# Attention stage of a ViT tower: position products with the image innermost, GpSimd scaling the probabilities, a new order of TensorE's side jobs

## The reference

```python
qkv = (x @ qkv_w.T).reshape(b, n, 3, HEADS, HEAD_DIM).transpose(2, 0, 3, 1, 4)
q, k, v = (qkv[0], qkv[1], qkv[2])
attn = jnp.einsum('bhqd,bhkd->bhqk', q, k) * scale
r_p_k = tab_kv[iv] + tab_kh[ih]
attn = attn + jnp.einsum('bhqd,qkd->bhqk', q, r_p_k) * scale
attn = jax.nn.softmax(attn, axis=-1)
out = jnp.einsum('bhqk,bhkd->bhqd', attn, v)
r_p_v = tab_vv[iv] + tab_vh[ih]
out = out + jnp.einsum('bhqk,qkd->bhqd', attn, r_p_v)
out = out.transpose(0, 2, 1, 3).reshape(b, n, QKV_DIM)
return out @ proj_w.T + proj_b
```

## Time and profile before

| What | Value |
|---|---|
| median of 3 runs | 5148.42 us (5146.3 to 5152.68) |
| the profiled execution | 5149.14 us, its span 5147.4 us |
| TensorE busy | 4691.5 us, 91% of the span |
| VectorE, ScalarE, GpSimd busy | 3364.0, 2283.2, 562.3 us (65%, 44%, 11%) |
| mean granted TensorE clock | 0.954 of full speed |
| attention stage | from about 554 to 4034 us of the span |

### The profile page before, as it was taken

How to read it: one execution, slowest core, us unless ns; L and a number is a source line. 1 busy time by engine, 2 the same in 40 slices (tenths; PEclk the granted TensorE clock), 3 DMA queues, 4 the chain that set the end, 5 groups by cost and what they waited for, 6 DMA issues and landing times. The chain is left out here.

```text
span 5147.4 us, 91556 instructions
## 1 busy us (share of the span) xinstructions
PE 4691.5 (91%) x30810; PEld 4419.7 (86%) x30810; DVE 3364.0 (65%) x9549; ACT 2283.2 (44%) x6372; POOL 562.3 (11%) x530
## 2 busy tenths in 40 slices
PE   4775799899899989989989998998999699999999
PEld 4775599899889889989988998998999599999999
DVE  4555566666666766666666666676667477777776
ACT  2443555455555545545555555554554122222222
POOL 1122100000000000000000000000000133333333
PEclk8887799999999999999999999999999799999999
DMA  6452000000000000000000000000000100000000
GB/s 140 97 124 61 13 1 1 1 20 1 1 20 1 1 2 20 1 1 20 1 1 16 6 1 1 20 1 1 11 1 1 38 19 18 18 18 18 18 18 18
DMA packets 65157, 99.50 MB, mean 19 GB/s; under 512 B 3763, under 2 KB 60674, under 8 KB 61120
## 3 DMA queue, kind: packets, MB, share of 16 engines
q1 hardware_dynamic: 61312, 90.31, 7.0%
q0 software_dynamic: 944, 2.42, 0.3%
q10 hardware_dynamic: 2560, 2.36, 0.2%
HBM read 65.88 MB, written 29.20 MB: 18 GB/s over the span
## 5 line engine op out<-in xcount | busy, mean ns | idle before, releaser
L643 ACT ACTIVATE att_prob<-att_s,att_npeak 99x198 f32<-99x198 f32 x1536 | 640.1, 422 | 1221.4 <-DVE att_npeak L816 1175.5
L816 DVE TENSOR_REDUCE att_npeak<-att_s 99x2 f32<-99x396 f32 x768 | 436.0, 568 | 892.3 <-PE att_s L988 890.2
L971 PE MATMUL att_o<-att_probT,att_vx 99*96 99x198 f32 (+1 forms) x3072 | 683.2, 345 | 1.3 <-ACT att_probT L633 1.3
L988 PE MATMUL att_s<-att_kx,att_qx 96*99 96x198 f32 (+1 forms) x3072 | 657.4, 336 | 3.3 <-DVE att_xres L782 2.5
L1356 PE MATMUL ffn_y<-ffn_down,ffn_hidden 128*128 128x192 f32 x3564 | 634.8, 328 | 6.7 <-DVE ffn_acc L1268 4.8
L1356 PEld LDWEIGHTS ffn_y<-ffn_down,ffn_hidden 128*128 128x128 f32 x3564 | 585.6, 190 | 28.4 <-DVE ffn_acc L1268 27.4
L971 PEld LDWEIGHTS att_o<-att_probT,att_vx 99*96 99x96 f32 (+1 forms) x3072 | 509.5, 182 | 42.4 <-issue 32.7
L988 PEld LDWEIGHTS att_s<-att_kx,att_qx 96*99 96x99 f32 (+1 forms) x3072 | 517.1, 168 | 18.4 <-issue 4.4
L806 DVE TENSOR_SCALAR att_prob<-att_prob,att_total 99x198 f32<-99x198 f32 x1536 | 458.9, 342 | 26.9
L1134 POOL TENSOR_TENSOR ffn_hidden<-ffn_relu 128x384 f32<-128x384 f32 x462 | 379.4, 827 | 708.6 <-ACT ffn_relu L1163 400.2
L1163 ACT ACTIVATE ffn_relu<-ffn_h 128x384 f32<-128x384 f32 x231 | 113.3, 490 | 706.2 <-PE ffn_h L1345 705.9
(11 more groups left out here) (201 smaller groups left out, 9368.6 us busy)
## 6 DMA issues: line engine op xcount, KB each, us to landing
tok_pixels<-in_x SPq DMA_DIRECT2D x24, 1568.0 KB
ffn_hid<-hidden SPq DMA_DIRECT2D x34, 288.0 KB, 2.9
att_xres<-hidden SPq DMA_DIRECT2D x8, 1188.0 KB
hidden<-att_xres SPq DMA_DIRECT2D x8, 1188.0 KB
out_hidden<-ffn_acc SPq DMA_DIRECT2D x33, 288.0 KB, 2.3
hidden<-tok_rows SPq DMA_DIRECT2D x8, 1176.0 KB
att_oT<-in_L_attn_qkv_w ACTq DMA_DIRECT2D x1, 1536.0 KB, 11.4
tok_posb<-in_L_tok_pos_embedding POOLq DMA_DIRECT2D x1, 1176.0 KB, 42.6
```

Of the source, the lines that this page charges most:

```text
L643: ins = nc.scalar.activation(prob[:, i % 2, h, :], s_bank[i % 2][0:HALF, h * NTOK:(h + 1) * NTOK], ACT.Exp, bias=npeak[:, i % 2, h:h + 1], ...
L816: nc.vector.tensor_reduce(npeak[:, i % 2, :], s_bank[i % 2][0:HALF, 0:2 * NTOK].rearrange("p (h k) -> p h k", h=2), AX.X, ALU.max, negate= ...
L971: ins = nc.tensor.matmul(o_bank[j % 2][0:M, 0:NTOK], vx[:, p % 2, 2 * b + k, v0:v0 + M], probT[:, j % 2, k * NTOK:(k + 1) * NTOK], start=( ...
L988: ins = nc.tensor.matmul(s_bank[i % 2][0:HALF, h * NTOK:(h + 1) * NTOK], qx[0:K, p % 2, head, q0:q0 + HALF], kx[0:K, p % 2, head, b * NTOK ...
```

## The change

The kernel's parts that are edited, all in `attention_stage`:

- `q2` and `rx` now hold the image innermost (token 0 of 8 images, then token 1). ScalarE and VectorE write them at a distance of 8 values, `group_rhs` reads a grid row as 112 neighbours and a grid column as 14 runs of 8. The products lie in the bank in the same order, and the copies out of it (`by_image`, `by_image_cols`) read at distance 8.
- The table `tq` is padded from 64 to 72 columns.
- `scaled` becomes `inverted_sums`: VectorE only inverts; GpSimd scales both heads in one instruction. GpSimd's bias goes into 16 pieces, one behind the scaling in each of the first 16 steps of a group.
- ScalarE's `turned_out` comes ahead of the exponentials.
- `spread` orders the jobs anew and places them by a table of lengths, `COST`. The turns go between the Q and V jobs of the last unit, two of them into the unit before.
- `rowhot`, a helper of the setup, lies in the memory of `norm`.

```diff
-        tq = m.sb("tq", [128, NG, 64])
+        tq = m.sb("tq", [128, NG, WIDE])
...
-            return view(src, [[NTOK, GB], [step, n]], off)
+            return view(src, [[step * GB, n], [1, GB]], off * GB)
+
+        def by_image(src, n):
+            return view(src, [[1, GB], [GB, n]])
+
+        def by_image_cols(src, n):
+            return view(src, [[1, GB], [GB, SIDE], [SIDE * GB, n]])
...
+        COST = {"turn": [10] * TURN, "first": [9] * 8 + [8, 8, 8, 5] + [8, 8, 8, 4] + [18] * 4,
+                "last": [10, 9, 9, 6, 9, 9, 9, 5] + [7] * 8}
...
-                    jobs = f[:12] + l[:4] + f[12:14] + l[4:8] + f[14:17] + l[8:11] + f[17:] + l[11:]
...
-                    jobs = turns + f[:4] + l[:4] + f[4:9] + l[4:8] + f[9:14] + l[8:11] + f[14:17] + l[11:13] + f[17:] + l[13:]
...
+                if ending and not last:
+                    jobs = []
+                    for a in range(4):
+                        jobs += f(Q[a]) + (t(2 * a + 2) if a < 3 else []) + f(V[a]) + (t(2 * a + 3) if a < 3 else [])
+                    jobs += l(0) + f(R[0])
                 else:
+                    jobs = f(V[0], Q[0], V[1], Q[1], Q[2], V[2], Q[3]) + l(0) + f(R[0], V[3])
+                jobs += l(1) + f(R[1], K[0]) + l(2) + f(R[2]) + l(3) + f(R[3], K[1])
+                jobs += l(4) + f(C[0], K[2]) + l(5) + f(C[1]) + l(6) + f(K[3], C[2]) + l(7, 8) + f(C[3])
+                jobs += l(9, 10, 11, 12) + (t(0) if turning else []) + l(13, 14) + (t(1) if turning else []) + l(15)
+                begin = 5 if ending and last else 0
+                costs = [COST[kind][j] for kind, _, j in jobs]
                 for k, job in enumerate(jobs):
-                    between[p * UNIT + begin + k * (UNIT - begin) // len(jobs)].append(job)
+                    between[p * UNIT + begin + sum(costs[:k]) * (UNIT - begin) // sum(costs)].append(job)
...
+                def group(g, s):
+                    for i in range(STEPS):
+                        pool.wait_ge(inverted, g * STEPS + i + 1)
+                        nc.gpsimd.tensor_tensor(prob[:, i % 2, :, :], prob[:, i % 2, :, :],
+                                                view(total[:, i % 2, :], [[1, 2], [0, NTOK]]), ALU.mult).then_inc(probs, 1)
+                        if i < TILES:
+                            if i == 0:
+                                pool.wait_ge(norm_made, (g + 1) * TURN)
+                            ins = nc.gpsimd.tensor_tensor(xres[:, s, i, :], xres[:, s, i, :], pbias[:, :], ALU.add)
...
-                        nc.scalar.activation(q2[:, cols], bank[:, 0:HC], ACT.Copy, scale=SCALE)
+                        nc.scalar.activation(view(q2[:, :], [[1, HC // NTOK], [GB, NTOK]], j * HC // NTOK),
+                                             bank[:, 0:HC].rearrange("p (b n) -> p b n", n=NTOK), ACT.Copy, scale=SCALE)
...
+                        if v != "first" or i >= 2:
+                            turned_out(n, i)
                         act.wait_ge(peaks, n + 1)
...
-                        if v != "first" or i >= 2:
-                            turned_out(n, i)
...
-                    nc.vector.tensor_copy(rx[ext:ext + 32, p % 2, cols], o_bank[j % 2][ext:ext + 32, 0:NTOK]
+                    nc.vector.tensor_copy(view(rx[ext:ext + 32, p % 2, :], [[GB, NTOK]], b), o_bank[j % 2][ext:ext + 32, 0:NTOK]
...
-                    st.did(nc.vector.reciprocal(total[:, j % 2, :], total[:, j % 2, :]))
-                    st.settle()
-                    for h in range(2):
-                        ins = nc.vector.tensor_scalar(prob[:, j % 2, h, :], prob[:, j % 2, h, :],
-                                                      total[:, j % 2, h:h + 1], None, ALU.mult)
-                    ins.then_inc(probs, 1)
+                    nc.vector.reciprocal(total[:, j % 2, :], total[:, j % 2, :]).then_inc(inverted, 1)
```

More of the change, by code:

```diff
@@ L350, in attention_stage @@
     EXT = 32
+    WIDE = 72
     NG = 30
@@ L451, in spread, with t, f, l @@
             for p in range(PAIRS):
-                f = first_jobs(p + 1) if p + 1 < PAIRS or not last else []
-                l = last_jobs(p - 1) if p or not first else []
-                if p + 1 < PAIRS:
-                    jobs = f[:12] + l[:4] + f[12:14] + l[4:8] + f[14:17] + l[8:11] + f[17:] + l[11:]
-                    begin = 0
-                elif last:
-                    jobs, begin = l, 5
-                else:
-                    jobs = turns + f[:4] + l[:4] + f[4:9] + l[4:8] + f[9:14] + l[8:11] + f[14:17] + l[11:13] + f[17:] + l[13:]
-                    begin = 0
+                ending, turning = p + 1 == PAIRS, p + 2 == PAIRS and not last
+                def t(*js):
+                    return [("turn", NEXT, j) for j in js]
+                def f(*js):
+                    return [("first", p + 1, j) for j in js] if not ending or not last else []
+                def l(*js):
+                    return [("last", p - 1, j) for j in js] if p or not first else []
+                Q, K, R, C, V = (range(n, n + 4) for n in (0, 4, 8, 12, 16))
+                if ending and not last:
[3 more added lines that the diff above has]
+                    jobs += l(0) + f(R[0])
+                else:
+                    jobs = f(V[0], Q[0], V[1], Q[1], Q[2], V[2], Q[3]) + l(0) + f(R[0], V[3])
[4 more added lines that the diff above has]
+                costs = [COST[kind][j] for kind, _, j in jobs]
                 for k, job in enumerate(jobs):
-                    between[p * UNIT + begin + k * (UNIT - begin) // len(jobs)].append(job)
+                    between[p * UNIT + begin + sum(costs[:k]) * (UNIT - begin) // sum(costs)].append(job)
             return between
@@ L566, in _ @@
                 pool.wait_ge(consts_in, 16 * 5)
+                def group(g, s):
[7 more added lines that the diff above has]
+                            ins = nc.gpsimd.tensor_tensor(xres[:, s, i, :], xres[:, s, i, :], pbias[:, :], ALU.add)
+                            if i == TILES - 1:
+                                ins.then_inc(resid_made, 1)
                 with pool.Fori(0, GROUPS // 2) as pair:
                     for s in range(2):
-                        pool.wait_ge(norm_made, (pair * 2 + s + 1) * TURN)
-                        nc.gpsimd.tensor_tensor(xres[:, s, :, :], xres[:, s, :, :], view(pbias[:, :], [[0, TILES], [1, DIM]]),
-                                                ALU.add).then_inc(resid_made, 1)
+                        group(pair * 2 + s, s)
             @block.scalar
@@ L755, in job @@
                             ins = nc.vector.tensor_tensor(
-                                dst, view(bank[src:src + 32, :], [[n * SIDE, GB], [1, SIDE], [SIDE, n]]), dst, ALU.add)
+                                dst, by_image_cols(bank[src:src + 32, :], n), dst, ALU.add)
                     elif kind == "last" and j < 4:
@@ L772, in job @@
                         ins = nc.vector.tensor_tensor(
-                            dst, view(bank[:, :], [[n * SIDE, GB], [1, SIDE], [SIDE, n]]), dst, ALU.add)
+                            dst, by_image_cols(bank[:, :], n), dst, ALU.add)
                     elif kind == "last":
@@ L981, in group @@
                         if i % UNIT == 0:
-                            all_read(base, v, "first", p, FIRST - 1)
+                            all_read(base, v, "first", p, max(range(FIRST), key=lambda j: order[v]["first", p, j]))
                         K = 128 if head else 96
```

36 lines of the change are left out of this document (17 added, 19 removed).

## The result

The changed kernel takes 5074.59 us (median of 4 runs, 5065.28 to 5083.04) against 5147.36 us (4 runs, 5143.08 to 5152.68): ratio 0.9859, interval 0.9846 to 0.9871, so 73 us or 1.4% less. The forecast was 4990, 158 us less; the sign and the range held, the size was twice too large. The profiled execution took 5078.64 us, its span is 5076.9.

The account below looks back on a forecast made before the run. TensorE's own path of work, waits and clock was taken to bound the attention stage. Savings of 113 us in plain units, 43 in turn units and 5 elsewhere, less 3, gave 158 off 5149.1: 4990 us, range 4740 to 5090.

Parts of the forecast that it names:

- Image innermost: Position products on TensorE: column products fall from 0.195 to 0.10 us each, 5.1 us less a unit.
- writes into the bank become one run everywhere: Products' writes into PSUM become contiguous; no cost was given for strided writes into q2 and rx.
- 72 columns: Weights wider than 64 on TensorE: slower entry into five product runs goes, 0.9 to 1.0 us a unit.
- GpSimd scales: Scaling leaves VectorE, which loses 0.56 us a step; GpSimd's product takes 0.86 us, 3 us lost in all.
- rival 2: VectorE's normalises in the turns wait for GpSimd's product: 96 us at most, 5087 us in all; chance 0.07.
- ScalarE's order: Copy of transposed values ahead of the exponentials: ScalarE's jobs start 0.15 us later in a step.
- The plain unit: Sixteen attention steps without turns: 59.9 us of work plus 5.4 of waits, 65.3, saving 2.9 us each.
- named third-job waits: In a plain unit, jobs standing third or fourth wait for bank copies, 0.3 to 1.1 us each, 5.4 together.
- The unit ahead of the turns: The unit before the last of a group: two turns moved into it cost 0.7 us.
- The turn unit: Last unit of a group: work 62.0, waits 1.85, 8.1 and 6.5, sum 78.5, with the clock 85 us.
- The charge of 6.6 us for the clock: Turn unit: three gaps of 2.7 us lower the clock, charged 2.2 us each, half of 4.4.
- Rival 1: TensorE stays fed, earlier copies or full clock: plain units 62.0, turn units 70, 4758 us in all; chance 0.19.

Follow-up runs that it names:

- the filled unit: The changed kernel with eleven extra fp32 products ahead of each of Q1, Q2 and Q3 in the unit with the turns: 5052.93 us, 0.9813.
- plain writes: The changed kernel with q2 and rx written by image in one run, so its products read permuted tokens: 5003.00 us, 0.9725.
- the first two turns uncounted: The changed kernel with cost 0 for the first two turns in the table that deals jobs to steps: 5049.63 us, 0.9828.
- wait-free order: The changed kernel with jobs from a table, mostly two a step in a plain unit, turns spread over both last units: 4765.56 us, 0.9268.

## Why the prediction was right and wrong

- **Image innermost: right in its price, a cost missed.** 0.095 us a product for my 0.10, 0.195 before. That runs of 8 values go like one run is what follows from the rule on the page "SBUF — State Buffer" of the Trainium skill, under "cachelines"; the trace agrees. The step that failed is "writes into the bank become one run everywhere": I followed the writes into PSUM and not those into q2 and rx, which got the stride that the reads lost. This cost of 0.40 us a Q and 0.16 us a step had no term. Taking it away gives 5003 us, 13 from my 4990, and unit by unit 64.7 (forecast 65.3), 69.1 (66.0) and, as the mean of the six middle groups, 84.8 (85).
- **72 columns: right**, 1.0 us a unit, 29 us in all of 46, since the turn unit's clock took part of the rest.
- **GpSimd scales: right in size, not in weight.** 846 ns for 0.86; VectorE's normalises take 381 ns each (380 before), so the 96 us of rival 2 are not there, and the blocked scalings are gone with their instruction. The lock of the Trainium skill's page "SBUF — State Buffer", under "shared port pair", costs nothing that these rows show now. The bias pieces take 0.59 us, not 0.42, which nothing waits for. I never priced what the changed kernel would be without it: 207 us more.
- **ScalarE's order: wrong to leave it at 0.15 us of shift.** In the changed kernel it costs 29 us, through the last two units of a group.
- **The plain unit: right.** Each of the named third-job waits is there, within 0.35 us, and the sum missed by 0.5 us, less than the missed writes cost (1.1): the other terms were together too high by some 0.6.
- **The unit ahead of the turns: wrong.** I charged two turns, 0.7 us. It takes 4.6 to 5.8 us over a plain one: VectorE's normalises and low halves in front of its additions, the V job that slid into third place, and some clock.
- **The turn unit: waits right, clock wrong.** Q behind its turn waits 2.25 us (forecast 2.7), V0 2.4 (1.85), the later third jobs 6.3 together (6.5). The 78.5 us of work and waits are near the estimate of 79 at full clock from the filled unit. The charge of 6.6 us for the clock, half of 4.4 for each gap and so half a guess, was the term that failed: the six middle units average 91.3, some 12 above that estimate, about one of it the wait without a releaser. With plain writes they average 84.8, which the charge fits; most of the excess is thus a price of the missed writes. The unit took 84.06 us at a clock of 0.94 and 95.95 at 0.80, with the same waits. With shorter copies or filled waits no clock under 0.91 is left in the six groups; with ScalarE's old order one of 0.86 is, and with the first two turns uncounted one of 0.83. So all four make the low clock rarer, and only the first two kept it away in all six groups.
- **Rival 1** (4758, TensorE stays fed) fell for this order. The wait-free order comes to its time (4766) with the change's other parts, but partly by luck: the attention stage gained more than the rival says, and the experts stage lost over 80 us.

Of the 85 us missing, the strided writes explain 72 by experiment, about half of it by way of the turn unit and its clock. The remaining 13 us are a difference of medians and can't be placed: the profiled execution with plain writes took 4980 us, 10 under the forecast. In it the unit ahead of the turns is 3.1 us dearer than forecast in seven groups, 22 us, and 39 plain units 0.3 to 0.6 us cheaper cancel most of that. Why the clock takes one value or another in equal units is open.

## What to carry to other kernels

Before a product is made faster, look at what waits beside it: with two banks, a third job in a step pays for the copy out of the first, and a shorter product only shows more of that wait. When a layout is turned for a reader, price the writer too, on its own engine. Order the jobs last, after the durations have changed, and put third jobs behind long ones: here that was worth more (309 us) than the whole change (73 us). And read the stages that you did not edit too: here 87 us of a gain were lost in one of them.

## What was not expected of the hardware

- A copy out of PSUM whose fp32 results lie 32 bytes apart in SBUF takes ScalarE 903 ns instead of 502 (128 x 396) and VectorE 522 instead of 359 (32 x 198). Reading PSUM with that distance cost nothing: ScalarE takes 540 ns for 32 x 448 where it took 541 with runs of 14, VectorE's addition of 32 x 448 631 ns where it took 629.
- Adding 33 products to the turn unit made it 13.5 us shorter in one group, where the granted clock stayed at 1.00 instead of 0.80, and 5.0 us on the average of six.
- The same instructions of an unedited stage took 1203 us instead of 1117 in three of the kernels, with waits of VectorE that have no releaser in the profile.
